# Attention–FFN kernel on Trainium2: two copies of the second attention's normalised rows, one of the last stage's, and scores in 32x64 tiles without the masked quarter

## The reference, cut to what matters

```python
x = x + attn_a(layernorm(x), Wq, Wk, Wv, Wo, bo)
x = x + ffn(layernorm(x), rhs)
x = x + attn_b(layernorm(x), q_w, k_w, v_w, Wq, Wk, g_w, ...)
x = x + ffn(layernorm(x), rhs)

# attn_a, 16 heads of 64: linear attention, causal
q, k = relu(x @ Wq) + EPS, relu(x @ Wk) + EPS
attn = q . cumsum(k v^T) / (q . cumsum(k)), then @ Wo + bo
# ffn: rows and rhs rounded to whole numbers of -127..127, product, scaled back
# attn_b, 16 heads of 32, rank 16
q, k = rope(x @ q_w.T), rope(x @ k_w.T)
q_r, k_r = q . Wq[h], k . Wk[h]              # 32 -> 16 per head
g = sigmoid(x @ g_w.T + g_b)
M_t = decay * M_(t-1) + (g_t * k_t * scale) v_t^T
y_t = q_t . M_t ; out = y @ out_w.T + out_b
result = layernorm(x + out) * ln_g + ln_b
```

## Time and profile before

| | |
|---|---|
| median of 3 runs | 3157.41 us (3151.66 to 3161.16) |
| the profiled execution | 3157.9 us, span 3156.2 us |
| PE busy | 3020.7 us, 96% of the span |
| PE weight loads busy | 2280.0 us, 72% |
| DVE, ACT, POOL busy | 2311.1, 711.4, 997.9 us (73%, 23%, 32%) |
| chain that ended last | PE 94%, DVE 3%, DMA 1% |
| mean granted clock of TensorE | 0.987 of full speed |

### The profile page before, as it was taken

One profiled execution on the slowest core, in us unless ns is written; L12 is line 12 of the kernel. 1 busy time (PEld: TensorE's weight loads), 2 busy tenths in 40 slices (PEclk: granted clock), 3 DMA queues, 4 the chain that ended last, 5 costly groups with the idle time before them and its releaser, 6 DMA issues.

```text
span 3156.2 us, 117197 instructions
## 1 busy us (share of the span) xinstructions
PE 3020.7 (96%) x50710; PEld 2280.0 (72%) x50836; DVE 2311.1 (73%) x5280; ACT 711.4 (23%) x1229; POOL 997.9 (32%) x1397
## 2 busy tenths in 40 slices
PE   3699999999999999999999999999999999999985
PEld 3577777777777777777777777777777777777764
DVE  6777777777777777777777777777777777777764
ACT  2222222222222222222122122222222222222211
POOL 2033333333333333333333333333333333333333
PEclk9899999999999999999999999999999999999997
DMA  4222222122222222222222222222222222222210
GB/s 169 67 41 47 45 47 51 38 48 51 37 48 51 41 44 51 42 44 50 44 47 44 44 47 45 45 46 45 45 46 46 50 40 48 50 37 48 50 34 27
DMA packets 384337, 152.96 MB, mean 48 GB/s; under 512 B 352800, under 2 KB 361632, under 8 KB 383904
## 3 DMA queue, kind: packets, MB, share of 16 engines
q1 hardware_dynamic: 383904, 146.02, 23.5%
HBM read 45.29 MB, written 16.78 MB: 20 GB/s over the span
## 4 chain that ended last, share of the span: by engine, by line
PE 94%; DVE 3%; DMA 1%; issue 1%; ACT 0%; POOL 0%; SPq 0%; DVEq 0%; POOLq 0%
PE bank L718 22%; PE bank L720 21%; PE bank L719 21%; PE bank L1008 7%; PE bank L891 3%; PE bank L844 3%; PE bank L800 3%; PE bank L676 3%; PE bank L960 2%; PE bank L818 2%; PE bank L863 2%; PE bank L983 2%; PE bank L970 1%; PE bank L996 1%; DVE absmax L1146 1%
## 5 line engine op out<-in xcount | busy, mean ns | idle before, releaser
L718 PE MATMUL bank<-xaT,wq_hi 128*128 128x128 f16 x2048 | 363.1, 221 | 5.0 <-DVE wk_lo L1171 4.0
L718 PE MATMUL bank<-xbT,wb 128*128 128x128 f16 x2048 | 350.7, 220 | 13.6 <-DMA xbT<-work 13.6
L719 PE MATMUL bank<-xaT,wq_hi 128*128 128x128 f16 x2048 | 362.6, 221 | 0.0
L720 PE MATMUL bank<-xaT,wq_lo 128*128 128x128 f16 x2048 | 362.6, 221 | 0.0
L718 PE MATMUL bank<-xaT,wk_hi 128*128 128x128 f16 x2048 | 360.3, 220 | 0.0
L719 PE MATMUL bank<-xaT,wk_hi 128*128 128x128 f16 x2048 | 360.1, 220 | 0.0
L720 PE MATMUL bank<-xaT,wk_lo 128*128 128x128 f16 x2048 | 360.0, 220 | 0.0
L719 PE MATMUL bank<-xbT,wb 128*128 128x128 f16 x2048 | 350.6, 220 | 0.0
L720 PE MATMUL bank<-xbT,wb 128*128 128x128 f16 x2048 | 350.6, 220 | 0.0
L638 POOL TENSOR_TENSOR work<-work 128x512 f32<-128x512 f32 x128 | 162.8, 1272 | 487.2 <-DVE work L1401 487.2
L1434 DVE TENSOR_TENSOR work<-bank,causal 128x512 f32<-128x512 f32 x256 | 159.0, 684 | 142.8 <-PE bank L960 142.8
(11 more groups left out here) (207 smaller groups left out, 7928.1 us busy)
## 6 DMA issues: line engine op xcount, KB each, us to landing
xin<-in_L_attn_a_x SPq DMA_DIRECT2D x64, 256.0 KB, 2.6
out<-xf SPq DMA_DIRECT2D x64, 256.0 KB, 2.5
table<-in_tables SPq DMA_DIRECT2D x64, 192.5 KB, 3.0
work<-in_L_attn_a_Wq SPq DMA_DIRECT2D x1, 2048.0 KB, 8.9
work<-in_L_attn_a_Wk SPq DMA_DIRECT2D x1, 2048.0 KB, 14.4
wb<-in_L_attn_a_Wv SPq DMA_DIRECT2D x1, 2048.0 KB, 19.0
work<-in_L_attn_a_Wo SPq DMA_DIRECT2D x1, 2048.0 KB, 8.5
work<-work SPq DMA_TRANSPOSE x128, 3.1
```

The source lines that it names most:

```text
L718: nc.tensor.matmul(o, a[0], b[0], start=first, stop=False)
L719: nc.tensor.matmul(o, a[0], b[1], start=False, stop=False)
L720: return nc.tensor.matmul(o, a[1], b[0], start=False, stop=last)
```

## The change

Four things are changed together.

1. `xnb` has two copies and `nb_ap` waits for `no_f` of two chunks earlier. `xf1` has one copy and `nf1_ap` waits until the output of the chunk before it has been sent.
2. `sb` makes its scores in quarters of 64 keys by 64 queries: 48 matmuls of 32x64 tiles over 64 columns, 12 for each group of 32 partitions, the quarter with all keys behind all queries left out. For the second half of the heads (`j` = 1) the two halves of the keys are swapped on the partitions, so that the heads of both halves use both columns of tiles evenly. `kr_e` therefore writes `khat` in three pieces (128x128, 2 of 64x128) and `vb_e` writes `vbs` in three (128x256, 2 of 64x256) instead of one. The mask has a second form, and the four banks of `sb` are cleared once at the start.
3. Several waits on the same bank are merged into one (`take_behind`, `all_filled`).
4. ORDER, BANK, LATE, BORROWED and COUNTS are new: the same steps with other lags, in another order.

```diff
-ORDER = [("qr_e", 4), ("xhb", 4), ("sb", 4), ("ys", 4), ("mm1_e", 5), ("sb_e1", 4), ("qk2", 1), ("ub", 4), ("sb_e0", 4),
...
-         ("aT1_h", 1), ("qr", 3), ("kT", 3), ("qk1", 0), ("aT0_t", 1), ("mm0_e", 2), ("kT_e", 3)]
...
+ORDER = [("no_f", 5), ("ld_t", 4), ("oa1", 2), ("nf1_st", 5), ("gb_e", 4), ("nf1_rs", 5), ("oa0", 2), ("nf0_q", 3),
...
+         ("so0", 1), ("no_ap", 4), ("ub_a", 4), ("nf0_ap", 2), ("v1_e", 1), ("so1", 1)]
...
-    (0, "qr_e"): ("load o",),
+    (0, "no_f"): ("load o",),
     (0, "qk0_e"): ("max o", "all o", "turn decay"),
-    (1, "wo_e"): ("scale o", "hi o", "keep decay"),
-    (1, "rnd1"): ("lo o", "load rhs", "load bk"),
...
+    (1, "kt0_e"): ("scale o", "hi o", "keep decay"),
+    (1, "qT0_t"): ("lo o", "load rhs", "load bk"),
...
+    def take_behind(self, units, read):
+
+        last = {}
+        for u in units:
+            last[BANK[u]] = max(last.get(BANK[u], (0, -10 ** 9)), self.uses(u), key=lambda n: n[1])
+        for u, back in read:
+            if self.exists(back):
+                per, const = self.uses(u, back)
+                last[BANK[u]] = max(last.get(BANK[u], (0, -10 ** 9)), (per, const + 1), key=lambda n: n[1])
+        for b, n in last.items():
+            self.wait(self.empty[b], n)
+        return [(self.ps[BANK[u]], self.full[BANK[u]]) for u in units]
...
-        xnb = sb("xnb", [P, D])
+        xnb = sb("xnb", [P, 2, D])
...
-                    pair = [c.take(f"o{g}a"), c.take(f"o{g}b")]
-                    c.done(f"u{g}", 1)
-                    c.done(f"qk{2 * g}")
-                    c.done(f"qk{2 * g + 1}")
+                    pair = c.take_behind((f"o{g}a", f"o{g}b"), ((f"u{g}", 1), (f"qk{2 * g}", 0), (f"qk{2 * g + 1}", 0)))
...
-                for j in range(2):
-                    for odd in range(2):
+                places = [[(j, odd, q) for j in range(2) for odd in range(2) for q in (0, 1) if q >= key_half(j, place)]
+                          for place in range(2)]
+                for n in range(6):
+                    for place in range(2):
+                        j, odd, q = places[place][n]
+                        at = tile(2 * j + odd).start + HALF * q
                         for l, (bank, f) in enumerate(four):
                             h = slice(32 * l, 32 * l + 32)
-                            last = nc.tensor.matmul(bank[:, tile(2 * j + odd)], khT[h, odd, j, :], qh[h, j, :],
-                                                    start=True, stop=True)
-                            if j == 1 and odd == 1:
+                            last = nc.tensor.matmul(bank[half_of(place), at:at + HALF], khT[h, odd, j, half_of(place)],
+                                                    qh[h, j, half_of(q)], start=True, stop=True, skip_group_check=True)
+                            if n == 5 and place == 1:
                                 last.then_inc(f, 1)
...
-                nc.scalar.activation(vbs[:, :], bank[:, :], ACT.Copy, scale=unscale[:, SBV:SBV + 1]).then_inc(e, 1)
+                one = unscale[:, SBV:SBV + 1]
+                nc.scalar.activation(vbs[:, 0:256], bank[:, 0:256], ACT.Copy, scale=one)
+                for place in range(2):
+                    h = half_of(key_half(1, place))
+                    last = nc.scalar.activation(vbs[half_of(place), 256:512], bank[h, 256:512], ACT.Copy, scale=one[h, :])
+                last.then_inc(e, 1)
...
             def nf1_ap(c):
-                c.wait(out_free[c.par], c.half(2, each=16))
-                normalise("f1", c, xwb[:, c.par, :], xf1[:, c.par, :])
+                c.wait(out_free, c.count(1, each=16))
+                normalise("f1", c, xwb[:, c.par, :], xf1[:, :])
...
             def nb_ap(c):
-                c.wait(x3_ready, c.count(1))
-                normalise("b", c, xwb[:, c.par, :], xnb[:, :])
+                c.wait(x3_ready, c.count(2))
+                normalise("b", c, xwb[:, c.par, :], xnb[:, c.par, :])
...
-                nc.vector.tensor_tensor(khat, bank[:, 0:HB * R], gate[:, :], ALU.mult).then_inc(khat_ready, 1)
+                nc.vector.tensor_tensor(khat[:, 0:P], bank[:, 0:P], gate[:, 0:P], ALU.mult)
+                for place in range(2):
+                    h = half_of(key_half(1, place))
+                    last = nc.vector.tensor_tensor(khat[half_of(place), P:2 * P], bank[h, P:2 * P], gate[h, P:2 * P], ALU.mult)
+                last.then_inc(khat_ready, 1)
...
-                        nc.vector.tensor_tensor(scb[:, l, :, :], four(bank), causals[:, 0:1, :].to_broadcast([P, 4, P]),
-                                                ALU.mult).then_inc(e, 1)
+                        nc.vector.tensor_tensor(scb[:, l, :, :].rearrange("p (j o) t -> p j o t", j=2),
+                                                bank[:, :].rearrange("p (j o t) -> p j o t", j=2, o=2),
+                                                causals[:, :, None, :].to_broadcast([P, 2, 2, P]), ALU.mult).then_inc(e, 1)
...
-            for b in sorted({BANK[u] for u in ("s0a", "s0b", "s1a", "s1b")}):
+            for b in sorted({BANK[u] for u in ("s0a", "s0b", "s1a", "s1b", "sb0", "sb1", "sb2", "sb3")}):
```

More of the change, by code:

```diff
@@ L102 @@
 LATE = {
[L103 removed]
+    (0, "no_f"): ("load o",),
     (0, "qk0_e"): ("max o", "all o", "turn decay"),
[L105 to L114 removed]
[10 rows of a table removed]
+    (1, "kt0_e"): ("scale o", "hi o", "keep decay"),
+    (1, "qT0_t"): ("lo o", "load rhs", "load bk"),
+    (1, "wo0"): ("max rhs", "all rhs"),
+    (1, "nb_st"): ("columns of rhs", "rows of rhs"),
+    (1, "sb_e1"): ("scale rhs",),
+    (1, "yb"): ("max bk", "all bk"),
+    (1, "xhb"): ("scale bk", "hi bk"),
+    (1, "xTa_h"): ("round rhs", "load bq"),
[12 rows of a table added]
 }
 TAKEN = ("q", "k", "v", "o", "rhs", "bk", "bq", "g", "bv", "rk", "rq")
[L129 to L138 removed]
+BORROWED = {"decay": (0, "qk0_e", 0),
+            "o": (0, "qk0_e", 2),
+            "rhs": (1, "wo0", 2),
+            "rhs rows": (1, "nb_st", 4),
+            "bk": (1, "yb", 1),
+            "bq": (2, "nf1_rs", 7),
+            "g": (2, "o1_e", 0),
+            "bv": (2, "mm0", 5),
+            "rk": (2, "wo0", 0),
+            "rq": (2, "nb_st", 6)}
 def borrowed_before(bank, slot, place):
@@ L237, in filled, with all_filled @@
             self.wait(self.full[BANK[unit]], (per, const + 1))
+    def all_filled(self, units, back):
+        if self.exists(back):
+            last = {}
+            for u in units:
+                last[BANK[u]] = max(last.get(BANK[u], (0, -10 ** 9)), self.uses(u, back), key=lambda n: n[1])
+            for b, (per, const) in last.items():
+                self.wait(self.full[b], (per, const + 1))
+    def take_behind(self, units, read):
+        last = {}
+        for u in units:
+            last[BANK[u]] = max(last.get(BANK[u], (0, -10 ** 9)), self.uses(u), key=lambda n: n[1])
+        for u, back in read:
+            if self.exists(back):
+                per, const = self.uses(u, back)
[3 more added lines that the diff above has]
+        return [(self.ps[BANK[u]], self.full[BANK[u]]) for u in units]
     def done(self, unit, back=0):
@@ L361, in hybrid_kernel @@
         block16 = xwb[:, 1, 256:384].rearrange("p (h i) -> p h i", h=HALF_H)
-        rhs_max = xf1[:, 0, :]
-        rhs_inverse = xf1[:, 1, :]
+        rhs_max = xnb[:, 0, :]
+        rhs_inverse = xnb[:, 1, :]
         rhs_cols = sb("rhs_cols", [P, KD])
@@ L500, in st_o @@
                 c.wait(out_ready, c.count())
-                sp.dma_start(at(out, c), xf1[:, c.par, :]).then_inc(out_free[c.par], 16)
+                sp.dma_start(at(out, c), xf1[:, :]).then_inc(out_free, 16)
             def transpose(n, to, src):
@@ L1086, in xTb_h @@
                 c.wait(xhat["b"], c.count())
[L1087 to L1090 removed]
+                c.all_filled(("kr", "qb", "kb", "vb", "gb"), 1)
+                nc.scalar.activation(xb_split[:, 0, :], xnb[:, c.par, :], ACT.Copy).then_inc(hi_done["xTb"], 1)
             def gb_s(c):
@@ L1489, in _ @@
                           wo_e=wo_e, nf0_st=nf0_st, nf0_ap=nf0_ap, nf0_q=to_int(0),
-                          mm0_e=mm_e(0), nb_st=nb_st, nb_ap=nb_ap, xTb_l=rest("xTb", xnb[:, :], xb_split),
+                          mm0_e=mm_e(0), nb_st=nb_st, nb_ap=nb_ap, xTb_l=rest_b,
                           qb_e=turn_parts("q", turn_q, cross_q), kb_e=turn_parts("k", turn_k, cross_k),
```

110 lines of the change are left out of this document (41 added, 69 removed), and 59 rows, old and new, of tables (COUNTS, LATE, ORDER).

## The result

The changed kernel takes 3325.26 us (median of 4 runs, 3324.73 to 3326.05), the kernel before 3157.84; the ratio is 1.0536, with a 95% interval from 1.0522 to 1.055. It is 5.4% slower. The forecast was 1.0% faster, 3126 us with a range from 3096 to 3160: wrong in sign, and outside the range.

What follows compares the result with a forecast made beforehand. PE's own instruction list was taken to bound the kernel. Scores −23, form changes −11, edge +12, registers +5, start −6 and tail −8 sum to −31: 3126 us, range 3096 to 3160.

Steps and rivals of the forecast that it cites:

- The loop's edge: PE at the loop's branch, now behind so1: 0.7 us open instead of 0.27, +12 us, bounds 0 and +16.
- an edge above a us: Sign of being wrong: PE's hole at the loop's edge exceeds a us, where some 0.7 was expected.
- The scores: sb and ys on PE: smaller matmuls on eight tiles save 0.36 us a chunk, −23 us; bounds −29 and +27.
- the rounds: In sb, twelve rounds of 64 columns on eight tiles set the time: 0.71 to 0.79 us, taken as 0.80.
- the records set the pace: Rival for sb: 96 records take 1.58 us as in s; 3176 us, deciding from 13 ns a record; 8%.
- Changes of form: PE's stretches of small tiles between projections and transposes fall from four to three: −11 us, bounds 0 and −16.
- registers: PE's added register and ISA operations in each loop iteration, a quarter of them uncovered: +5 us, bounds 0 and +20.
- the edge and the registers cost nothing: Rival: both are free and PE's 15.7 us without a record in the steady stretch go too; 3094 us; 12%.
- Start: Before the first chunks: o's scale and parts come about 11 us earlier, half counted, −6 us; bounds −13 and +3.
- Tail: Last chunk: nb_ap runs ahead of out_e, closing a PE hole; −8 us, bounds −13 and −3.
- DVE and ACT: kr_e to 870 ns and vb_e to about 1143, +0.45 and +0.46 us per chunk, hidden under PE.
- The new wait in the slot: Rival: PE waits half a us in each chunk at kr or sb, +32, no change at 3158 us; 13%.

Runs made afterwards that it cites:

- edge_pad110: The changed kernel with the loop's edge moved from before oa1 to before qk1 and 110 idle instructions at PE's start: 3129.08 us, 0.991 of the kernel before.
- after_pad192: The changed kernel with 192 idle instructions at the start of PE's list: 3272.53 us.
- edge_pad208: The changed kernel with the loop's edge moved to before qk1 and 208 idle instructions at PE's start: 3259.86 us in one execution.

## Why the prediction was wrong, point by point

**The step that failed** is "The loop's edge". It took the queue ahead of the sequencer for the only cover and a branch of 0.352 us with some short operations behind it for the whole cost, 0.7 us open and 0.9 as the upper bound: +12, at most +16. Measured are 7.6 us for each of 26 iterations, some 200. The 0.352 us of the earlier trace rows was not the price of a branch but that of a branch whose target had come in time, and no row of before showed the other price. For a branch whose target has come, the forecast's 0.7 us open at this place was near: 0.59 to 0.64 in the kernels with 64, 128 and 192 idle instructions. The prediction named "an edge above a us" as a sign of being wrong, and that is the sign that came. The queue's 0.42 us at the edge is right and beside the point. The instruction queue's row was on the page, and I didn't ask where in the program its packets fall.

**The scores**: −23 forecast, about −4 measured (0.06 us for 64 chunks). The pace is neither that of the rounds (0.80 us) nor that of `s` (1.58): `sb` takes 0.98 us for 92 records, 10.6 ns each:

```profile
1020.59 1.19 PE L987 MATMUL bank<-work 32*64 32x64 f32 x92
1021.57 0.29 PE L997 MATMUL bank<-work,state_b 32*64 32x128 f32 x1
```

So the term's size was wrong, since twelve rounds take longer than 0.71 to 0.79 us. The rival "the records set the pace" stayed short of the 13 ns at which it would have decided; whether the records or something else set the 10.6 ns was not tested. The prediction's estimate of 25 ns a record, one behind the other, rests on the 60 cycles of the Trainium skill, TensorEngine Tiling (Array Packing), section Instruction Overhead. The same row disagrees with it: 10.6 ns from record to record, so with eight tiles such overheads overlap at least in part.

**Changes of form, registers, holes elsewhere**: −11 and +5 forecast. They can't be told apart. With the tiles and the edge they sum to what lies between the 1st and the 60th `out` of edge_pad110: 2752.08 against 2771.34, −19. In the loop's steady slots 46.54 us stand against 46.98 to 47.00; the ten slots ahead of them are 3 us longer than before. Some 4 of the 19 are the tiles, and 11 are time in which PE has no record: 15.7 before, 4.5 now. That is the rival "the edge and the registers cost nothing" in part, and the forecast itself had no term for it. The forecast's −23 − 11 + 12 + 5 = −17 is close to −19, but it is made of other parts, so that it came out near is luck.

**Start**: −6 forecast, +5.7 measured in the changed kernel, +6.9 in edge_pad110. The weights are earlier, as forecast: the load of rhs is issued at 59.96 us, before at 71.71. But PE runs more work ahead of the first `out`, 2245 records against 2002, and is busy there for 6.1 us more. In edge_pad110 3.0 us of the 6.9 are idle instructions that PE's first wait doesn't cover. **Tail**: −8 forecast, −9.4 measured, −16.5 in edge_pad110 (167.4 us behind the 60th `out` against 183.9): PE is busy there for 131.7 us, before for 142.8. Together −9.6 in edge_pad110 against −14 forecast. In that kernel the sum is 2752.08 − 2771.34 = −19.3 between the 1st and the 60th `out`, +6.9, −16.5: −28.9, and the medians differ by 28.5.

**DVE and ACT** were hidden as forecast. `kr_e` has the price that was named; `vb_e` is longer, some 1.4 us instead of 1.14, with 470 ns for a piece of 64x256 where 381 were taken. The changed kernel's groups by shape:

```profile
L1127 ACT ACTIVATE vbs<-bank,unscale 64x256 f32<-64x256 f32 x128 | 60.1, 470 | 1.6
L1459 DVE TENSOR_TENSOR work<-bank,gate 64x128 f32<-64x128 f32 x128 | 36.8, 288 | 1.7
```

The new wait in the slot, the other rival of size, didn't come: no wait of PE for DVE or a transfer repeats from slot to slot in the changed kernel.

**Left open.** What the second copy of `xnb` is worth alone wasn't tried: with one copy, `nb_ap` of a chunk would wait in the new list for a `no_f` that stands behind it. Why the target lay at a block's start with 128 idle instructions is open as well, and so is what sets off a request. The packets themselves are in the trace, and each of the two holes shown ends 2.4 to 2.6 us after its packet begins (1042.89 to 1045.46, 1046.96 to 1049.38). But that a block is asked for on entering the one before it is worked out from where the holes are, and the kernel with 64 idle instructions doesn't fit it.

## What to carry to other kernels

When a loop's body is longer than a block of instructions and the engine never waits, look at the branch's row before and after a change, and at "issue" in the waits: 64 or 78 instructions more before the loop moved the time by 2 to 3% here, down in one kernel and up in the other, and such a difference says nothing about the change under test. What worked here was an edge with wide matmuls on both sides, the branch well into its block and the target at the start of its own. Compare two versions only with their branches equally placed. Small tiles cost not only their records: 256 instructions of them were used up sooner than the next 256 came.

## What the runs showed of the hardware

- The same loop, moved by idle instructions alone, took 3188 to 3325 us: single holes of up to 3.9 us. 256 idle instructions gave the changed kernel again. Sequential boundaries stall too, in dense f32 small tiles (1.74 us in `s`, 1.15 in `u`, after_pad192).
- Each return to the loop's head fetches the whole body again: 15, 14 or 13 packets of 16.4 KB an iteration. The branch took 3.2 us where its target's packet began 0.7 us behind it, and 0.37 us where it began 2.9 us ahead. Without the hint it took 3.7.
- With two holes at the edge (3.55 and 2.10 us, with 1.3 us of work between them) TensorE's granted clock fell to 0.50 as the second began and stayed there until 1054.0, for 6.4 us at least. With holes of 0.6 to 1.9 us far apart (edge_pad208) it was 0.990 in the mean.
- A semaphore increment on PE that nobody waits for takes 0.16 us (40.4 us for 256).
- With eight tiles of 32x64 at once, f32 records of 64 columns start 10.6 ns apart on average; with four tiles it is 15.
